# Closing normalisation of the feed-forward stage: feature sums by a GpSimd reduction over all partitions in place of two TensorE products of a split vector

## The reference, cut to what matters

```python
x = _L2_cond_ref(...)          # attention, then x + f_alpha * swiglu(...)

def _L3_cond_ref(input, convInfo, weight, bias, lin_w, lin_b):
    EPS = 1e-05
    mean = jnp.mean(input, axis=-1, keepdims=True)
    var = jnp.mean(jnp.square(input - mean), axis=-1, keepdims=True)
    out = (input - mean) * jax.lax.rsqrt(var + EPS) * weight + bias
    tar_bias = jnp.tanh(convInfo @ lin_w.T + lin_b)[:, None, :]
    out = out + tar_bias
    return out * weight + bias
```

## Time and profile before

| | |
|---|---|
| median of three runs | 1068.98 us (1066.23 to 1071.0) |
| profiled execution, span from first to last instruction | 1062.0 us |
| what lies around the span (median less span) | 7.0 us |
| PE busy | 1024.9 us, 97% of the span |
| DVE busy | 753.0 us, 71% |
| ACT busy | 637.4 us, 60% |
| POOL busy | 176.2 us, 17%; nothing after 819 us |
| mean granted TensorE clock | 0.992 of full |

### The profile page before, as it was taken

The page is one execution under the profiler, slowest core; times in us unless marked ns, Lnnn a source line. Parts: engine busy times, 40 slices in busy tenths (PEclk is TensorE's granted clock), DMA queues, the critical chain, the costliest instruction groups (busy, mean ns, idle before and its releaser), DMA issues.

```text
span 1062.0 us, 16530 instructions
## 1 busy us (share of the span) xinstructions
PE 1024.9 (97%) x5397; PEld 636.6 (60%) x5397; DVE 753.0 (71%) x1211; ACT 637.4 (60%) x867; POOL 176.2 (17%) x203
## 2 busy tenths in 40 slices
PE   7999999999999999999999999999999999999996
PEld 6776667777543444434444444434487777878784
DVE  5867668888877877787877878789765466555654
ACT  5556323353376777786777777677753564555545
POOL 0000001221231233232333334021310000000000
PEclk9999999999999999999999999999999999999998
DMA  9978633215434353734445363634210000000001
GB/s 287 381 184 237 174 95 110 41 35 173 105 123 103 103 150 75 207 79 157 99 132 127 95 179 77 185 80 116 79 28 1 20 1 21 20 20 20 1 20 40
DMA packets 92041, 110.95 MB, mean 104 GB/s; under 512 B 47184, under 2 KB 57424, under 8 KB 90960
## 3 DMA queue, kind: packets, MB, share of 16 engines
q1 hardware_dynamic: 60736, 100.56, 32.4%
q10 hardware_dynamic: 31248, 9.65, 5.2%
HBM read 65.81 MB, written 33.03 MB: 93 GB/s over the span
## 4 chain that ended last, share of the span: by engine, by line
PE 68%; DVE 11%; ACT 5%; issue 4%; DMA 2%; ACTq 1%; SPq 1%; POOL 0%; DVEq 0%; POOLq 0%
PE st_ps L1766 13%; PE st_ps L1622 9%; PE mx_ps L1766 7%; PE av_ps L1604 7%; PE val_ps L1479 5%; PE gate_ps L1479 5%; DVE mx L1196 5%; PE misc_ps L1535 4%; PE misc_ps L1642 3%; PE mx_ps L1559 3%; PE misc_ps L1655 2%; PE y_ps L1489 2%; DVE stage L1205 2%; PE misc_ps L1646 1%; DVE xres L1389 1%
## 5 line engine op out<-in xcount | busy, mean ns | idle before, releaser
L1196 DVE TENSOR_REDUCE mx<-mx_ps 128x1 f32<-128x512 f32 x488 | 314.4, 684 | 101.1 <-PE mx_ps L1559 99.5
L1559 PE MATMUL mx_ps<-kring,qring 48*128 48x512 f32 x500 | 199.7, 461 | 4.2 <-DVE mx L1196 2.2
L1622 PE MATMUL st_ps<-qring,kring 50*128 50x512 f32 x512 | 186.7, 444 | 3.5 <-ACT shared L919 3.4
L1622 PEld LDWEIGHTS st_ps<-qring,kring 50*128 50x128 f32 x512 | 76.2, 184 | 146.2 <-issue 112.1
L919 ACT ACTIVATE pbuf<-st_ps 128x1024 f32<-128x1024 f32 x128 | 129.3, 1023 | 41.7 <-PE st_ps L1622 40.1
L919 ACT ACTIVATE shared<-st_ps 128x1024 f32<-128x1024 f32 x128 | 127.9, 1021 | 38.2 <-PE st_ps L1622 37.3
L1559 PEld LDWEIGHTS mx_ps<-kring,qring 48*128 48x128 f32 x500 | 84.7, 183 | 31.0 <-DVE mx L1196 26.0
L1373 DVE TENSOR_TENSOR shared<-st_ps,shared 128x512 f32<-128x512 f32 x64 | 44.1, 689 | 80.4 <-PE st_ps L1766 61.8
L1043 ACT ACTIVATE p_hi<-shared 128x512 fp32r<-128x512 f32 x64 | 40.4, 631 | 71.8 <-DVE shared L1373 71.2
L1259 DVE SCALAR_TENSOR_TENSOR h<-val_ps,r,gelu 128x1024 f32<-128x1024 f32 x32 | 41.0, 1282 | 47.9 <-PE val_ps L1479 47.9
L1382 DVE TENSOR_TENSOR p_lo<-shared,p_hi 128x512 fp32r<-128x512 f32 x64 | 45.1, 705 | 37.7 <-ACT p_hi L1043 37.0
(11 more groups left out here) (239 smaller groups left out, 2062.9 us busy)
## 6 DMA issues: line engine op xcount, KB each, us to landing
chunk<-in_gen_w SPq DMA_DIRECT2D x8, 2048.0 KB, 9.2
qring<-q_parts SPq DMA_DIRECT2D x64, 192.0 KB, 3.5
kring<-k_parts SPq DMA_DIRECT2D x64, 192.0 KB, 4.6
q_parts<-stage SPq DMA_DIRECT2D x16, 512.0 KB, 2.9
k_parts<-stage SPq DMA_DIRECT2D x16, 512.0 KB, 2.8
xres<-in_xT SPq DMA_DIRECT2D x8, 512.0 KB, 11.5
shared<-in_x SPq DMA_DIRECT2D x8, 512.0 KB, 12.3
q_parts<-stage SPq DMA_DIRECT2D x16, 256.0 KB, 3.0
```

The source lines that it names most:

```text
L1196: nc.vector.tensor_reduce(mx[h // GH % 2][:, col:col + 1], mx_ps[:, qt % 2], AX, ALU.max).then_inc(S["mx_free"], 1)
L1559: nc.tensor.matmul(out, qring[h // GH][r:r + QROWS, h % GH // 2, qt * P:(qt + 1) * P], kring[h // GH][r:r + QROWS, h % GH // 2, :], start= ...
L1622: ins = nc.tensor.matmul(st_ps[half][:, kt % 2], kring[g][r:r + SROWS, i % GH // 2, kt * P:(kt + 1) * P], qring[g][r:r + SROWS, i % GH // ...
```

## The change

Both feature sums of batches 0 to 6 are made by GpSimd's `partition_all_reduce`: it reads `xsum` (128 partitions by 512 columns), sums over all 128 partitions and writes the sum to all partitions of a new tile, `mean_all` or `var_all`. The split copies, the four matmuls and `mean_r` go. `d` is now one `scalar_tensor_tensor` with -1/256 as its scalar, and Ln gets its 1/256 as its scale. VectorE waits for `var_all` of the batch before where it writes `xsum` again. The last batch's own normalisation stays as it was.

```diff
@@ gpsimd, after its last attention step
+            for b in range(1, NB):
+                wait_ffn(pool, "added", 2 * b - 1)
+                wait_ffn(pool, "d", b - 1)
+                nc.gpsimd.partition_all_reduce(mean_all[:], xsum, P, bass.bass_isa.ReduceOp.add) \
+                    .then_inc(F["mean_all"], 1)
+                wait_ffn(pool, "added", 2 * b)
+                wait_ffn(pool, "ln", b - 1)
+                nc.gpsimd.partition_all_reduce(var_all[:], xsum, P, bass.bass_isa.ReduceOp.add) \
+                    .then_inc(F["var_all"], 1)
@@ scalar
-            act.wait_ge(A["consts"], 2)
-            nc.scalar.activation(mean_r[:], mean_w[:], ACT.Copy)
...
-                    if f in (2, 5) and ends:
-                        wait_ffn(act, "added", 2 * b - 1 + f // 5)
-                        nc.scalar.activation(sum_hi[:], xsum, ACT.Copy).then_inc(F["sum_hi"], 1)
...
-                        wait_ffn(act, "stat", 2 * b)
-                        nc.scalar.activation(rstd, av_ps[:], ACT.Ln, bias=eps5[:]).then_inc(F["ln"], 1)
+                        wait_ffn(act, "var_all", b)
+                        nc.scalar.activation(rstd, var_all[:], ACT.Ln, bias=eps5[:], scale=1.0 / D) \
+                            .then_inc(F["ln"], 1)
@@ vector
-                    if f in (2, 5) and ends:
-                        wait_ffn(dve, "sum_hi", 2 * b - 1 + f // 5)
-                        nc.vector.tensor_tensor(sum_lo[:], xsum, sum_hi[:].bitcast(F32), ALU.subtract) \
-                            .then_inc(F["sum_lo"], 1)
...
                     if f == 1 and ends:
                         wait_ffn(dve, "x4", KD * b)
+                        wait_ffn(dve, "var_all", b - 1)
                         nc.vector.tensor_tensor(xsum, x_of(b - 1, 0), x_of(b - 1, 1), ALU.add) \
...
-                        wait_ffn(dve, "stat", 2 * b - 1)
-                        nc.vector.tensor_tensor(d, x_all(b - 1), both(av_ps[:]), ALU.subtract).then_inc(F["d"], 1)
+                        wait_ffn(dve, "mean_all", b)
+                        nc.vector.scalar_tensor_tensor(out=d, in0=both(mean_all[:]), scalar=-1.0 / D,
+                                                       in1=x_all(b - 1), op0=ALU.mult, op1=ALU.add) \
+                            .then_inc(F["d"], 1)
@@ tensor
-                    if f in (2, 5) and ends:
-                        if isinstance(b, int) and b == 1:
-                            wait(pe, "oaug", NG * NB)
-                        wait_ffn(pe, "sum_lo", 2 * b - 1 + f // 5)
-                        nc.tensor.matmul(av_ps[:], mean_r[:], sum_lo[:], start=True, stop=False)
-                        nc.tensor.matmul(av_ps[:], mean_r[:], sum_hi[:], start=False, stop=True) \
-                            .then_inc(F["stat"], 1)
```

More of the change, by code:

```diff
@@ L133, in all_stages @@
         cond_diag = sb(ctx, "cond_diag", [P, 2, NB])
-        mean_r = sb(ctx, "mean_r", [P, P], F32R)
         ident = sb(ctx, "ident", [P, P])
@@ L246, in all_stages @@
         p_lo = [at(f"p_lo{i}", [P, L], F32R) for i in range(4)]
-        sum_hi = at("sum_hi", [P, L], F32R)
-        sum_lo = at("sum_lo", [P, L], F32R)
+        mean_all = at("mean_all", [P, L])
+        var_all = at("var_all", [P, L])
         silu = [shared[:, n * L:(n + 1) * L] for n in range(2)]
@@ L293, in all_stages @@
             "w_hi w_lo t h gate_done silu hid_done pf p_hi p_lo out_step "
-            "xb x4 added sum_hi sum_lo stat d sq ln rstd e fin stored").split()}
+            "xb x4 added mean_all var_all stat d sq ln rstd e fin stored").split()}
         block = ctx.enter_context(nc.Block())
@@ L1067, in _ @@
             for hh, cs in halves:
-                wait_ffn(act, "stat", 2 * NB + 1 + hh)
+                wait_ffn(act, "stat", 3 + hh)
                 nc.scalar.activation(rstd[:, cs], stat[hh][:, cs], ACT.Ln, bias=eps5[:]).then_inc(F["ln"], 1)
@@ L1407, in _ @@
                         normalise(b + 1, 1 - par, (2, 4, 5).index(f))
+            wait_ffn(dve, "var_all", NB - 1)
             for hh, cs in halves:
@@ L1421, in _ @@
             for hh, cs in halves:
-                wait_ffn(dve, "stat", 2 * NB - 1 + hh)
+                wait_ffn(dve, "stat", 1 + hh)
                 nc.vector.tensor_tensor(d[:, :, cs], xres[:, NB - 1, :, cs], both(stat[hh][:, cs]), ALU.subtract) \
@@ L1833, in _ @@
                 ins.then_inc(F["out_step"], 1)
+            wait(pe, "oaug", NG * NB)
             for hh, cs in halves:
```

## The result

The changed kernel took 1059.26 us (median of four runs, 1052.60 to 1060.28) against 1069.99 us for the kernel before on the same chip (1066.23 to 1073.44): a ratio of 0.9891, interval 0.9854 to 0.9927. It is faster by about 1.1%. The forecast was 1100 us and slower.

A forecast was written before the change was run, and what follows sets the result against it. TensorE was taken to bound the kernel before, the chain through GpSimd after. Five batches at 4.5 us (22.5), 2.5 for the last and 6 for the first made 31 us: 1069 to 1100 us, range 1057 to 1227.

The forecast's parts named there:

- The pace of the steady batches: Feed-forward stage: eight steps with nothing but products on TensorE take 32.6 us a batch, against 34.47 us before.
- T: Time of one GpSimd reduction of 128 by 512, two a batch: bounded by 1.3 and 19.7 us, taken as 6.
- first rival: The reduction is short or the port isn't held, so TensorE stays the bound: 1058 us, chance 0.27.
- 27 + 2T: Length in us of one batch's chain with the port held; 39 us at T = 6, 4.5 more than before.
- the port held: VectorE's operations with two SBUF inputs and this `tensor_scalar` stand still beside a reduction, costing VectorE its whole length.
- break-even rival: T between 3.2 and 3.9 with the port held, or first-batch exchange eating the gain: 1069 us within 5, chance 0.07.
- The chain: From a batch's gate product through `xsum`, mean, `d`, variance and Ln to SiLU, before the next batch: 25.8 + 2T.
- The first batch: Its mean can't start before L704 ends and GpSimd's routines are exchanged; set at 6 us in all.
- late first mean: Cost of the delayed mean at the start of the feed-forward stage, about 2 us in the first rival's sum.
- The 7.0 us around the span: Difference between the profiled span of 1062.0 us and the median of 1069, added to the forecast span of 1093.
- cores in turn: GpSimd's cores work nearly one after another: 1185 us at T = 12, 1293 at T = 19.7; chance 0.17.
- columns not streamed: Each column passes core after core before the next begins: above 1290 us, some 1840 at T = 59; chance 0.05.

The follow-up runs named there:

- no_sums: The changed kernel without the sums over the partitions for batches 0 to 6, `d` and Ln reading `xsum` itself: 1054.3 us, ratio 0.9872 to the kernel before.
- one_long: The changed kernel with each reduction reading `xsum` twice, 1024 columns in one instruction, half the result unused: 1088.11 us, ratio 1.019 to the kernel before.
- twice: The changed kernel with one more reduction of `xsum`, its result unused, ahead of each of the fourteen: 1081.77 us, ratio 1.0101 to the kernel before.
- again: The changed kernel run once more, unaltered: 1059.87 us against 1068.0 for the kernel before, ratio 0.9918.
- first_on_te: The changed kernel with batch 1's two sums made by TensorE as before, GpSimd starting with batch 2: 1055.65 us, ratio 0.9892 to the kernel before.
- first_on_te_routines_back: The changed kernel with batch 1's sums on TensorE and a small GpSimd `tensor_tensor` at the end restoring the first library: 1057.64 us, ratio 0.9878.
- routines_back: The changed kernel with a small ordinary GpSimd `tensor_tensor` at the end, bringing back the first library: 1057.55 us, ratio 0.9893 to the kernel before.

## Why the prediction was wrong

**The pace of the steady batches: right.** 32.6 us for a batch of nothing but products was forecast, 32.65 measured in after and in `no_sums`.

**The cost of a reduction: wrong, and this moved the forecast to slower.** The step "everything overlaps except the four steps over lanes, which one core makes for every column, and one handing back, 4 x 1.28 + 0.8 = 5.9, so T = 6" failed. T is 3.23 us for 512 columns (3.40 beside the second `xsum`) and 6.12 for 1024, so 5.6 ns a column and some 0.35 us fixed. That is 2.5 plain two-input passes. The choice within 1.3 to 19.7 was made by a picture of how the work is cut, and not by a row. The nearest row was the plain pass at 1.28 us, and the first rival's own condition was "hardly over two of GpSimd's plain passes". The break-even point of the forecast, T = 3.7, was only 2.3 us from the T that I took and 0.4 us from the true one; so the chances of slower (0.66) and faster (0.26) leaned on an estimate that no row supported. The right T alone would not have given the right answer: the forecast's 27 + 2T is 33.6 us at T = 3.3, above TensorE's 32.6, and T of 3.2 to 3.9 with the port held is the condition of its own break-even rival, 1069 us. That the kernel got faster took a chain shorter than written, too.

**The port: right in kind, too long in size.** `p_lo` 1.58 and 3.87 us, `ffn_hi` 2.86 and 5.16: it is held, and by the reduction's length. But the forecast took from the earlier trace rows that VectorE starts again at GpSimd's end. In after, `p_lo` without its own 0.69 us started again 1.13 us before the recorded end, in `one_long` 1.73 us before. The Trainium skill (SBUF — State Buffer, section "Who interferes with whom") has the lock held for the whole instruction. These traces agree that it holds beside a partition reduction (`p_lo` 1.58 us, and 0.69 in `no_sums`), but VectorE gets on before its recorded end.

**The chain: right in its links, some 2 to 3 us too long.** `one_long` is the test, since T is there what was assumed. The forecast was 27 + 2T; with 6.12 and 6.28 that is 39.4 us, measured 36.58. The rest of the chain is 24.2 us, not 25.8 to 28.3. Two links were shorter. From the mean's end to the end of `d` it took 942.91 - 939.49 = 3.4 us and not 5.3; from the variance's end to the end of SiLU 920.22 - 915.64 = 4.6 us and not 6.2, since the held work had got on before the reduction's recorded end. From `d` to the variance it took 3.0 us and 3.1 was forecast. The link from the gate product to the end of `xsum` took 13.0 us (920.27 to 933.28) and not 11.2. Had T been 6, the time would have been `one_long`'s 1088 us and not 1100: inside the forecast's own range, and slower. At the true T the chain is at most about 24.2 + 6.6 = 30.8 us, an estimate from the constant of `one_long`; it lies under 32.65, and nothing of it shows. The trace of after agrees: the SiLU that the chain ends with is done at 975.15, and the gate product that needs it starts at 977.21, 2.06 us later. (The 3 to 4 us read from after and `twice` are more, since VectorE got on between the two reductions there.)

```profile
977.21 0.39 PE L1771 MATMUL mx_ps<-ffn_hi,gate_lo 128*128 128x512 f32 x1
```

**The first batch: two terms too small, which cancel in part.** The forecast priced the sums at 1.83 us in every batch; in batch 1 they cost TensorE 4.15 us, so 14.1 us were to be gained and not 12.8. The first rival took 2 us off for the late first mean; it cost 5.8. The stage gained the difference, about 8.3 us, where that rival had 10.8; so the late first mean was sized wrong, and so was the gain. The medians gained 10.7 us in the first comparison and 8.1 in `again`, so that the rival's 1058 us came so near 1059.26 is in part luck. The exchange is 5.88 us of idle time, and the Trainium skill (GPSIMD Engine Reference, section 2.1) agrees with its figure of about 6 us for the first call into freshly loaded code. The forecast's sum by this figure added 5 us to the 6 us of the first batch. `one_long` has a T of 6.1, and its batch 1 takes 44.92 us, 7.2 more than the 37.77 of a batch 1 with sums on TensorE: 6 was near, and 11 would have been too much.

**The rest.** The copies, subtractions and the new form of `d` (1.22 us, as the earlier trace rows) cost nothing on the path: right. The 7.0 us around the span were no property of a launch: 2.1 us lie around it in after, and the other 5 or so are the difference between a profiled execution at clock 0.992 and the median. Of the rivals, the first one came true in its time, 1058 us, and in its sign, batches 32.6 us apart. Its conditions did not: the port is held, and with it held it wanted a T of at most 2.8. The slow ones, cores in turn and columns not streamed, are out by T. Of the signs named, a held `p_lo` (1.58 us, not over 2) and the gap before the first mean were seen; idle time of TensorE in each batch, Ln waiting for GpSimd, and batches of 38 to 50 us were not.

## The best version

`first_on_te` and `first_on_te_routines_back`, at 1055.65 and 1057.64 us, are below the changed kernel's 1059.26 and 1059.87, with a stage that is 1.5 to 1.6 us shorter. In the medians the first lies only 1.4 us above `no_sums` (1054.3), but the stage of `no_sums` is 4.15 us shorter. The medians mix in the granted clock, which was lower in the executions of `no_sums` (0.981 to 0.990) than in those of `first_on_te` (0.981 to 0.994). So up to 4 us are left to gain, all in batch 1. Whether the whole program is faster than after by the 1.6 us isn't settled, since one kernel's executions lie up to 13 us apart.

## What to carry to other kernels

Before work goes from the engine that bounds to an idle one, work out the break-even duration of the new operation; where the estimate comes out near it and rests on a picture of the inside, not on a row, the chances should be near even. A new operation may be long as long as its chain stays under the bounding engine's lead, so compare chain and pace, and not duration and duration. Price the first and the last turn of a loop by themselves; here batch 1 paid 4.15 us for its sums on TensorE and a steady batch 1.8. Give GpSimd's first call of a new kind a stretch in which nobody waits for it.

## What the runs showed of the hardware

- `partition_all_reduce` over 128 partitions in fp32: 3.23 to 3.40 us for 512 columns, 6.11 to 6.28 us for 1024.
- VectorE's `p_lo`, with two SBUF inputs, and its `tensor_scalar` `ffn_hi` stand still beside it (1.58 and 2.86 us, without reductions 0.69 and 0.88), but go on 1.13 us (512 columns) or 1.73 us (1024) before its recorded end. In `twice`, with two reductions back to back, VectorE got on between them.
- An exchange of GpSimd's routines is a gap of 5.88 us with no instruction (5.71 in `routines_back`), and a program that ends on other routines than it began with pays 7.6 us once more at its start. `routines_back` shows that one last ordinary instruction avoids it.
